# Mask products ahead of the score products, a load behind six writes, and experts moved into the last sequence's tail

## What is computed

```
q, k, v = x @ wq + bq, x @ wk + bk, x @ wv + bv      # rotary on q and k
scores  = q k^T / sqrt(8) + causal mask;  attn = softmax(scores)
x1 = layernorm(x + (attn v) @ wo + bo)
idx = argmax(softmax(x1 @ wg));  location = count of earlier tokens of that expert
keep the token if location < 512
x2 = layernorm(x1 + gate * (x1 @ W[idx]^T + b[idx]) if kept, else layernorm(x1))
```

## Time and profile before

| | |
|---|---|
| Median of 3 runs | 452.92 us (452.65 to 453.24) |
| Profiled execution | 455.94 us, span of the trace 454.3 us |
| Busy share of the span | PE 90%, PEld 79%, DVE 70%, ACT 38%, POOL 45% |
| Mean granted clock | 0.947 of full speed |

### The profile page before, as it was taken

How to read it: one execution, slowest core, us unless ns; L and a number is a source line. 1 busy time by engine, 2 the same in 40 slices (tenths; PEclk the granted TensorE clock), 3 DMA queues, 4 the chain that set the end, 5 groups by cost and what they waited for, 6 DMA issues and landing times. The chain is left out here.

```text
span 454.3 us, 10445 instructions
## 1 busy us (share of the span) xinstructions
PE 408.6 (90%) x3270; PEld 360.2 (79%) x3270; DVE 316.4 (70%) x814; ACT 173.4 (38%) x377; POOL 202.9 (45%) x376
## 2 busy tenths in 40 slices
PE   4455698999999999999999999999999999999942
PEld 4344596989899888989898989898898888897831
DVE  5566644668687887877787868686877877765563
ACT  7541133343443433443434343443434433334300
POOL 6264233342535445364646363635455465251313
PEclk9956596999999999999999999999999999999958
DMA  5299663927659593939393958777595849600000
GB/s 141 73 193 144 109 95 79 151 59 131 99 118 124 121 119 96 152 84 157 88 146 88 147 88 150 91 136 102 122 123 130 103 120 122 94 11 23 13 0 24
DMA packets 145827, 47.29 MB, mean 104 GB/s; under 512 B 104349, under 2 KB 142113, under 8 KB 145802
## 3 DMA queue, kind: packets, MB, share of 16 engines
q1 hardware_dynamic: 139898, 42.65, 59.3%
q10 hardware_dynamic: 5184, 2.36, 2.9%
q0 software_dynamic: 720, 1.97, 1.5%
HBM read 30.70 MB, written 14.68 MB: 100 GB/s over the span
## 5 line engine op out<-in xcount | busy, mean ns | idle before, releaser
L934 PE MATMUL ps_pv<-probs,v_diag 128*128 128x64 f32 (+3 forms) x1024 | 191.3, 323 | 2.9 <-ACT probs L544 2.5
L934 PEld LDWEIGHTS ps_pv<-probs,v_diag 128*128 128x128 f32 x1024 | 148.8, 193 | 11.9 <-ACT probs L544 6.0
L544 ACT ACTIVATE probs<-ps_ab 128x512 f32<-128x512 f32 (+1 forms) x176 | 97.8, 559 | 153.2 <-PE ps_ab L898 148.6
L725 DVE TENSOR_REDUCE row_max<-ps_ab 128x2 f32<-128x512 f32 (+3 forms) x176 | 108.0, 631 | 21.8 <-PE ps_ab L898 21.8
L922 PE MATMUL ps_ab<-k_plain,q_diag 128*128 128x64 bf16 (+3 forms) x512 | 67.2, 244 | 13.3 <-DMA q_diag<-plain_parts 9.2
L913 PE MATMUL ps_ab<-q_plain,k_diag 128*128 128x64 bf16 (+3 forms) x512 | 65.5, 236 | 0.0
L922 PEld LDWEIGHTS ps_ab<-k_plain,q_diag 128*128 128x128 bf16 x512 | 36.0, 102 | 23.9 <-issue 8.7
L711 DVE TENSOR_REDUCE y_sel<-ps_m 128x128 f32<-128x1024 f32 x31 | 37.8, 1219 | 16.2 <-PE ps_m L887 16.2
L437 POOL COPY v_diag<-v_rows 64x128 f32<-64x128 f32 x64 | 18.4, 288 | 65.6 <-PE ps_pv L934 33.9
L898 PE MATMUL ps_ab<-mask_a_bf,ident_bf 128*128 128x128 bf16 (+2 forms) x176 | 44.9, 255 | 0.0
L898 PE MATMUL ps_ab<-mask_b_bf,ident_bf 128*128 128x128 bf16 (+2 forms) x176 | 43.2, 246 | 0.0
(11 more groups left out here) (156 smaller groups left out, 718.3 us busy)
## 6 DMA issues: line engine op xcount, KB each, us to landing
plain_parts<-rot SPq DMA_DIRECT2D x180, 64.0 KB, 2.0
k_plain<-plain_parts SPq DMA_DIRECT2D x16, 384.0 KB, 3.9
q_diag<-plain_parts SPq DMA_DIRECT2D x32, 192.0 KB, 5.4
q_plain<-plain_parts SPq DMA_DIRECT2D x16, 384.0 KB, 6.3
k_diag<-plain_parts SPq DMA_DIRECT2D x32, 192.0 KB, 6.7
x_in<-in_L_attn_x_dram SPq DMA_DIRECT2D x16, 128.0 KB, 5.9
x_res<-in_L_attn_x_dram SPq DMA_DIRECT2D x16, 128.0 KB, 3.1
out_dram<-y_out POOLq DMA_DIRECT2D x15, 128.0 KB, 2.5
```

The source lines that it names most:

```text
L544: act.activation(probs[:, k % PR, 0:cols], ps_b[k % 2][:, 0:cols], ACT.Exp, scale=SCALE)\
L725: last = dve.tensor_reduce(row_max[:, NBLK - 1 - j, groups[0]:groups[-1] + 1], scores[:, :, col:col + width(j)], AX.X, ALU.max)
L934: mm = pe.matmul(ps_pv[:, g // 4, BLK * j:S], v_diag[q][:, j, 128 * g:128 * g + 128], probs[:, k % PR, col:col + width(j)], start=(j == 0 ...
```

## The change

Four things. (1) `masks` now comes first in each chunk, with the flag that opens the accumulation, and the last score product releases the reader. (2) In step 0, SP's queue has the load of the third x behind the writes of parts 2 and 3. (3) In slot 10 the routing masks come ahead of the gate's sum, on all steps. (4) The experts of sequence 14, tile 0, go from slot 12 to slot 13 of step 16, behind the last PV products; tile 1 from slot 13 of step 16 to slot 5 of step 17, behind the output projection of sequence 15. Their selections go to slots 3 and 11 of step 17, and the addition to slot 11. For that the last sequence's x1 lies in `x_res`, its gate in a new `gate_last`, and both its expert tiles in `ps_ab`; the wait for `z2_done` is gone.

```diff
         def expert_bank(d, t):
-            return ps_ab[:, 0:2, :] if t == 1 and is_step(d, B - 1) else ps_m
+            return ps_ab[:, 2 * t:2 * t + 2, :] if is_step(d, B - 1) else ps_m
+        def x1_of(d):
+            return x_res if is_step(d, B - 1) else x1
+        def gate_of(d):
+            return gate_last if is_step(d, B - 1) else gate_kept
...
-                if has(n) and not is_step(s, -2):
+                if has(n) and not (is_step(s, -2) or is_step(s, 0)):
                     after(sp, "xt_ready", n)
                     sp.dma_start(x_in[:, :, :], of_seq(x_t, n)).then_inc(s_["x_loaded"], 16)
...
                     write(rot_2, 1, "rot2_done")
                     write(rot_3, 2, "rot3_done")
+                    if is_step(s, 0):
+                        after(sp, "xt_ready", n)
+                        sp.dma_start(x_in[:, :, :], of_seq(x_t, n)).then_inc(s_["x_loaded"], 16)
...
-                    if slot == 12 and has(d):
+                    if slot == 12 and has(d) and not is_step(s, B):
                         select(d, 0)
-                    if slot == 3 and has(e):
+                    if slot == 3 and is_step(s, B + 1):
+                        select(e, 0)
+                    if slot == (11 if is_step(s, B + 1) else 3) and has(e):
                         select(e, 1)
...
-                    if slot == (5 if is_step(s, B + 1) else 4) and has(e):
+                    if slot == (11 if is_step(s, B + 1) else 4) and has(e):
                         add_experts(e, z2)
...
                     if slot == 5 and has(d):
-                        if is_step(s, B + 1):
-                            after(dve, "z2_done", e, 1, 1)
                         after(dve, "rs1_done", d, 1, 1)
...
                     if slot == 10 and has(d):
-                        after(dve, "egate_done", d, 1, 1)
-                        dve.tensor_reduce(e_sum[:, :], e_gate[:, :, :], AX.X, ALU.add).then_inc(s_["gate_sum"], 1)
-                        after(dve, "gate_sum", d, 1, 1)
-                        dve.reciprocal(gate[:, :], e_sum[:, :]).then_inc(s_["gate_done"], 1)
-
                         after(dve, "loc_ready", d, 1, 1)
                         dve.tensor_scalar(route[0:E, :], ps_route, -1.0, BIG, ALU.add, ALU.mult)
...
+                        after(dve, "egate_done", d, 1, 1)
+                        dve.tensor_reduce(e_sum[:, :], e_gate[:, :, :], AX.X, ALU.add).then_inc(s_["gate_sum"], 1)
                         after(dve, "route_done", d, 1, 1)
                         dve.tensor_reduce(n_kept[:, :], kept[:, :, :], AX.X, ALU.add).then_inc(s_["nkept_done"], 1)
+                        after(dve, "gate_sum", d, 1, 1)
+                        dve.reciprocal(gate[:, :], e_sum[:, :]).then_inc(s_["gate_done"], 1)
...
-                return pe.matmul(v, ident_bf[:, :], rows, start=False, stop=True, skip_group_check=True)
+                return pe.matmul(v, ident_bf[:, :], rows, start=True, stop=False, skip_group_check=True)
...
-                        for i, (j, g, col) in enumerate(parts_of(CHUNKS[k])):
-                            pe.matmul(ps_b[k % 2][:, col:col + width(j)], diag_block(k_diag[q], g, j),
-                                      q_plain[q][:, g, BLK * j:S], start=(i == 0), stop=False, skip_group_check=True)
-                        masks(ps_b[k % 2], CHUNKS[k], mask_b_bf, False).then_inc(s_["b_ready"], 1)
+                        masks(ps_b[k % 2], CHUNKS[k], mask_b_bf, False)
+                        for j, g, col in parts_of(CHUNKS[k]):
+                            mm = pe.matmul(ps_b[k % 2][:, col:col + width(j)], diag_block(k_diag[q], g, j),
+                                           q_plain[q][:, g, BLK * j:S], start=False, stop=True, skip_group_check=True)
+                        mm.then_inc(s_["b_ready"], 1)
...
-                    if slot == 12 and has(d):
+                    if slot == 12 and has(d) and not is_step(s, B):
                         experts(d, n, 0)
...
-                    if slot == 13 and has(d):
+                    if slot == 13 and has(d) and not is_step(s, B):
                         experts(d, n, 1)
+                    if slot == 13 and is_step(s, B):
+                        experts(d, n, 0)
...
+                    if slot == 5 and is_step(s, B + 1):
+                        experts(d - 1, n, 1)
```

More of the change, by code:

```diff
@@ L174, in layer_kernel @@
         seen = sb("seen", [128, E], bf)
+        gate_last = sb("gate_last", [128, 2])
         kept, n_kept, gate_kept = sb("kept", [128, 2, E]), sb("n_kept", [128, 2]), sb("gate_kept", [128, 2])
@@ L703, in add_experts @@
                     after(dve, "gk_done", e, 1, 1)
-                    last = dve.scalar_tensor_tensor(out=z2[:, t, :], in0=y_sel[:, t, :], scalar=gate_kept[:, t:t + 1],
-                                                    in1=x1[:, t, :], op0=ALU.mult, op1=ALU.add)
+                    last = dve.scalar_tensor_tensor(out=z2[:, t, :], in0=y_sel[:, t, :], scalar=gate_of(e)[:, t:t + 1],
+                                                    in1=x1_of(e)[:, t, :], op0=ALU.mult, op1=ALU.add)
                 last.then_inc(s_["z2_done"], 1)
@@ L817, in step @@
                             .then_inc(s_["route_done"], 1)
+                        after(dve, "egate_done", d, 1, 1)
+                        dve.tensor_reduce(e_sum[:, :], e_gate[:, :, :], AX.X, ALU.add).then_inc(s_["gate_sum"], 1)
                         after(dve, "route_done", d, 1, 1)
                         dve.tensor_reduce(n_kept[:, :], kept[:, :, :], AX.X, ALU.add).then_inc(s_["nkept_done"], 1)
+                        after(dve, "gate_sum", d, 1, 1)
+                        dve.reciprocal(gate[:, :], e_sum[:, :]).then_inc(s_["gate_done"], 1)
                         after(dve, "nkept_done", d, 1, 1)
-                        dve.tensor_tensor(gate_kept[:, :], n_kept[:, :], gate[:, :], ALU.mult).then_inc(s_["gk_done"], 1)
+                        after(dve, "gate_done", d, 1, 1)
+                        dve.tensor_tensor(gate_of(d)[:, :], n_kept[:, :], gate[:, :], ALU.mult).then_inc(s_["gk_done"], 1)
                     if slot == 10 and is_step(s, -1):
@@ L920, in step @@
                         after(pe, "a_taken", t, NCH, max(k - (3 if is_step(t, 0) else 1), 0))
-                        for i, (j, g, col) in enumerate(parts_of(CHUNKS[k])):
-                            pe.matmul(maxima_bank(t, k)[:, col:col + width(j)], diag_block(q_diag[at], g, NBLK - 1 - j),
-                                      k_plain[at][:, g, 0:width(j)], start=(i == 0), stop=False, skip_group_check=True)
-                        masks(maxima_bank(t, k), CHUNKS[k], mask_a_bf, True).then_inc(s_["a_ready"], 1)
-                    if slot == 12 and has(d):
+                        masks(maxima_bank(t, k), CHUNKS[k], mask_a_bf, True)
+                        for j, g, col in parts_of(CHUNKS[k]):
+                            mm = pe.matmul(maxima_bank(t, k)[:, col:col + width(j)], diag_block(q_diag[at], g, NBLK - 1 - j),
+                                           k_plain[at][:, g, 0:width(j)], start=False, stop=True, skip_group_check=True)
+                        mm.then_inc(s_["a_ready"], 1)
+                    if slot == 12 and has(d) and not is_step(s, B):
                         experts(d, n, 0)
@@ L958, in step @@
                         for t in range(2):
-                            mm = pe.transpose(ps_n[:, 128 * t:128 * t + 128], x1[:, t, :], C("ident"))
+                            mm = pe.transpose(ps_n[:, 128 * t:128 * t + 128], x1_of(d)[:, t, :], C("ident"))
                         mm.then_inc(s_["x1t_ready"], 1)
```

2 lines of the change are left out of this document (1 added, 1 removed).

## The result

| | before | after |
|---|---|---|
| Median of 12 and 12 runs on one chip | 452.69 us (450.15 to 453.24) | 454.46 us (452.96 to 456.13) |
| Profiled execution, its span | 455.94, 454.3 us | 456.13, 454.5 us |

The ratio is 1.0049 [1.0033, 1.0065]: the changed kernel is slower by 0.5%, some 2.2 us. The forecast was 454.0 and +1.1. The profiled executions are single ones: that of before lies 3.25 us above its median here, that of after 1.67 us.

A forecast was written before the change was run, and what follows sets the result against it. TensorE alone was taken to bound the middle, with waits and queue order counting at both ends. Start +3.5, middle 0.0 and end -2.4 gave +1.1 on the 452.92 us median: 454.0 us, range 450.4 to 456.5.

The forecast's parts named there:

- rival 1: Start, SP queue: the third x does not come late, so only the end's gain stands, 450.5 us; chance 0.15.
- Start, +3.5: Step 0: x load behind six writes moves its transposes from 33.77 to 37.2, and nothing takes that up; bounds 3.3 to 4.8.
- everything behind is in TensorE's and VectorE's program order: Start, behind the third x's transposes: maxima, split, q and k, rotation, tables all shift, so 49.96 becomes 53.4.
- Masks, 0.0: Middle, mask products first: gains and losses of weight-load cover sum to -0.005 us a step, times 15; bounds -3.8 to +3.7.
- Rival 2: Middle, cover one way only: only gains, -3.8, 450.2 (chance 0.08), or only losses, +3.7, 457.7 (chance 0.07).
- Gate order, 0: Middle, VectorE's gate sums behind the routing: no time change, at most 0.4 us of cover lost in the tail.
- TensorE's fullness covers it: Middle: swapping two small VectorE operations with two others costs 0, since TensorE is busy throughout.
- a step shorter or longer by 0.1 us: Middle: a step length changed by this much or more would show the cover reckoning of the mask products wrong.
- End, -2.4: Last sequences, experts of the last but one moved: -1.85 - 0.85 + 0.1 + 0.2 us; bounds -2.9 to -0.2.
- -0.85 up to routing: End: full clock expected at transposes and logits, saving half of 0.70 + 1.03 us.
- rival 3: End: the clock stays at half, the end gives only 0.2, total 456.2 us; chance 0.15, counted within the forecast's 0.65.
- the removed experts: End: eight products of 0.23 us leave the place ahead of the last PV chunks, -1.85 us.

## Why the prediction came out as it did

The total came within 0.5 us by the medians (454.46 for 454.0) and within 1.1 by the ratio (+2.2 for +1.1, which is outside the measured [1.5, 2.9]). That it came so near is luck in good part: three of its terms were wrong, and their errors cancelled.

- **Start, +3.5: the mechanism right, the size too small.** The place in the queue was stuck and not the transfer (rival 1 is out); the writes were out at 34.82 (reckoned 34.8), x landed 2.3 us behind its issue (reckoned 2.3), the transposes came at 37.18 (37.2) with 3.18 us of idle time put down to x, and TensorE's third chunk at 53.07 (53.4). The runs say +3.6 and +5.4 (start alone, twice) and +5.8 (undone in place). The step that failed is the last one, "everything behind is in TensorE's and VectorE's program order", a shift by a fixed time: it was read from one profiled execution with 15.46 us from the transposes to the first maximum, where other kernels with x first take 13.3 to 13.8. At step 3 the changed kernel stands 3.09 behind that one execution of before, but 7.39 behind the same kernel with x first (107.47 against 100.08, single executions too). How much of the surplus is the clock stays open.
- **Masks, 0.0: prices right, places wrong.** Gaps of 0.03, 0.06 and 0.08 came as written. The failed step is the sum over slots, which took every gain and loss as a time of TensorE: the gains of slots 12 and 13 fall into the wait for ScalarE's exp, and without them the same sum is +0.109 a step, 1.6 us in fifteen. Measured +0.6 us alone (it can't be told from nothing) and about +1.1 in place. Rival 2 is out in both forms.
- **Gate order, 0: wrong.** "TensorE's fullness covers it" was read off busy times that cannot show a stop of 0.15 us, and in a step that has none. Measured -2.0 [-3.1, -1.0]. The sign that the forecast had named, a step shorter or longer by 0.1 us, could not show this error or that of the masks: the step went from 24.21 to 24.15, which is -0.17 of the gate order and +0.11 of the masks.
- **End, -2.4: right.** Measured -2.6 [-3.5, -1.7] alone. In the profiled pair -0.75 of the -0.85 up to routing came (11.39 against 12.14 from the sums on; the full clock held to the logits and rival 3 is out; the two transposes took 0.45 and the logits 0.63, not half of 0.70 and 1.03), and the removed experts gave about 1.5 (0.87 - 2.41 between the marks) in place of 1.85. Of the difference 0.08 is in the last PV group itself, 2.72 against the 2.64 of the earlier trace rows, which is the gap behind a 64-column product; the rest is not placed. Behind routing it was +0.08, not +0.3, and POOL's output, as reckoned, is what comes last.
- **Sum.** Measured 4.7 (the middle of 3.6 and 5.8) - 2.6 - 2.0 + 1.1 = +1.2 by parts, +2.2 [1.5, 2.9] for the whole; the two agree within the intervals of the parts. The forecast's +1.1 had the start short by about 1.2 and the masks by 1.1, and missed 2.0 of the gate order's gain and 0.2 of the end's: 1.2 + 1.1 - 2.0 - 0.2 = +0.1.

## What to carry over

In a queue that is held up, the next transfer pays the whole stop, here 3.4 us for the x load and as much for the first write, so the transfer that an engine waits for goes first, ahead of those that have slack. An engine that the profile calls full can still be stopped for a tenth of a microsecond in every step: compare the distance between the starts of two of its rows with what the work between them takes, and look at what the other engine read just before. A saving on a full engine counts only where the next thing in its program waits for nobody else; before summing gaps over a step, mark the points where it meets another engine. Read the middle from a step of the steady loop and not from the last ones, which lack some of the work. And follow a gain past the place where it arises: 1.7 us won at 50 us were 0.4 or less at 104.

## What the runs showed of the hardware

- The granted clock of one and the same stretch differs between executions, with and without a standstill. With the start edit alone it was 1.00 from 27 to 33 us and 0.50 from 36 to 43, behind 3.80 us of waiting; in its second execution 0.50 from 36 to 39 and 1.00 from 40 to 46; in the profile of before 0.50 from 30 to 39, with TensorE busy throughout from 30 to 36. The products of q and k took 2.7 us at the half clock (40.19 to 42.9) and 1.5 at the full one (39.72 to 41.3).
- A bf16 score product of 64, 128 or 192 columns ahead of a float32 product leaves a gap of 0.08, 0.06 or 0.03 us; one of 256 columns leaves none, and several in a row help no more than the last of them.
- Issuing writes right behind the operand loads takes 7.21 us for six, 4.26 for the first four and 1.18 for two more: the stop falls on whoever is first. An x load of 128 KB behind them is issued in 0.59 and lands after 2.3, where in first place it took 4.02 and 6.2.
- The row of a group of matmuls can hide a stop: 1.06 us for eight PV products of 128 columns stands both where the next products start 0.89 us and where they start 1.04 us behind.
